# Attention of a decoder layer: scores of four heads at once, scores and maxima taking turns on three pairs of PSUM banks

## The chip, the cores and the metric

The kernel runs on one core of a Trainium2 chip. The metric is the device time of one execution in microseconds (us).

## The reference

One decoder layer on a batch of four sequences of 512 tokens with 512 features, in fp32. `ctx` has 512 tokens of 256 features.

```
q, k, v = heads(x @ Wq), heads(x @ Wk), heads(x @ Wv)            # 16 heads of 32
std  = softmax(q k^T / sqrt(32)) v
qa, ka = affinities(q), affinities(k)                            # 8 splats per head
w    = (qa * amplitudes) ka^T;  w = w / (sum(w) + 1e-8)
attn = ((1 - blend) * std @ Wo) + blend * (w v) @ Wo
x = layernorm(x + attn)
x = layernorm(x + ssm(ctx, z = x))      # conv, x_proj, softplus, scan over 512 steps with 16 states, gate silu(x)
x = layernorm(x + ffn(x))               # ternary weights, silu(gate) * up, rms norm, down
```

The affinities are sums of two exponentials of a token's distance to eight positions per head. Because w factors, `w v` is computed as qa times (ka^T v), one small product over all keys ("the affinities' product", L1319), with a denominator of its own (L1333).

## The kernel before

The four sequences ("batches" 0 to 3) are worked through one after the other, each in an attention phase and an FFN phase. A setup ahead of them quantises the FFN's weights. The state space scan of batch b + 1 doesn't depend on the attention; it is cut into 32 halves (state n, channel half a) that are spread over the phases. A half is two decays `dA = exp(A delta)` on ScalarE (`exp_dA`, L529), a product with B (L810), the scan (L818) and a product with C (L821) on VectorE (`scan_half`, L802), and a DMA of GpSimd's queue that accumulates into YA (L445). `slot_halves` (L257) says after which key tile of which head group how many halves stand. Outside the first batch a group of heads has two halves, behind key tiles 1 and 3, group 3 has three; in the first batch groups 0 to 2 have 3, 3 and 4.

The attention goes by head groups j = 0 to 3 of four heads (32 rows of the array each), and in each by key tiles kt = 0 to 3 of 128 keys. For a key tile TensorE makes the scores of all 512 queries against the 128 keys, keys on partitions. Softmax needs the maximum of each query, which lies across partitions. So the scores are computed twice. The *maxima product* (`max_scores`, L1187, matmuls L1201) of group (j, g) puts the scores of 128 queries g against all keys, queries on partitions, into banks 0 to 3, one bank to a head, all four heads on the four row groups of the array. VectorE reduces the four banks in one operation (`max_groups`, L869, L873). When four groups g of a head group are done, `transpose_max` (L1205, matmul L1208) turns the maxima into rows in bank 0, and ScalarE copies them negated into BR (`bias_row`, L574). The *score product* (`score_pair`, L1211) then makes the scores of two heads in banks 4 and 5 (L1214), and a product of a row of ones with BR subtracts the maxima (L1218). ScalarE takes the exponential of both banks into PT (L649). The *values products* (`values`, L1222, L1230) accumulate PT times V in bank 6 and PT times ones in bank 7, each of the four heads in its own 32 columns. At the end of a head group ScalarE inverts the sum by a logarithm and an exponential (`inverse_start`, L591), and VectorE normalises (`normalise`, L875).

Each engine's order is written out by hand, and engines wait for each other by semaphores. TensorE's order in a key tile is: pair 0, perhaps a maxima product, values into bank 6 of the key tile before, pair 1, values into bank 7, perhaps a maxima product. A pair waits for the exponential of the pair before, since both use banks 4 and 5. A maxima product waits for the reduction before. `GROUPS` (L271) says how many maxima groups of head group j + 1 are done ahead of each key tile of group j:

```
GROUPS = {0: (1, 2, 3, 4, 4), 1: (0, 2, 3, 4, 4), 2: (0, 1, 3, 4, 4), 3: (0, 0, 0, 0, 0)}
```

Before key tile 0 of group 2 (`KV_GROUP`) comes the affinities' product: the keys' affinities are transposed at the end of group 0 (L1352, bank 1), copied by ScalarE at the start of group 1 (L638), multiplied with V behind the second pair of group 2 (L1319, bank 1) and masked by VectorE (`splat_kv`, L921), for which the next maxima product waits, since bank 1 is its bank too. In group 3 there are no maxima. There TensorE makes the denominator (L1333, bank 0), transposes the next batch's context (L1161), makes its input projection (L1170) and the splat products for all queries (L1346, banks 0 and 1).

## Time and profile before

| | us |
|---|---|
| median of 3 executions (1514.86 to 1522.54) | 1519.27 |
| the profiled execution | 1525.26 |
| its span, first to last instruction | 1523.5 |
| TensorE busy (matmuls) | 1288.5 |
| VectorE busy | 1172.2 |
| ScalarE busy | 753.9 |
| GpSimd busy | 162.7 |

PE is TensorE, PEld its weight loads, DVE is VectorE, ACT is ScalarE, POOL is GpSimd, SP is SyncE. L12 is line 12 of the kernel. A multiplication of fp32 operands shows as two matmul records; overlapping records are counted once as busy time. "ps" is PSUM. The granted clock is TensorE's, as a part of 2.4 GHz; it has two levels, 1.0 and 0.5, and a stretch shows their mean.

### The profile page before, as it was taken

How to read it: one execution, taken by the hardware profiler on the slowest of the kernel's cores; microseconds unless marked ns; L12 is line 12 of the kernel's file. 1: busy time of each engine (PE TensorE's matmuls, PEld its weight loads, DVE VectorE, ACT ScalarE, POOL GpSimd, SP SyncE). 2: the span in 40 equal slices, each digit the busy share in tenths (PEclk: the TensorE clock that was granted, in tenths of full speed). 3: DMA queues.
4: the chain of work that ended last, by engine and by line, in shares of the span. 5: the costliest groups of instructions: out<-in, count | busy, mean ns of one | idle time of the engine just before them, and what ended most of it. 6: DMA issues, size and time to landing. Idle time of an engine off the chain costs nothing.

```text
span 1523.5 us, 15252 instructions
## 1 busy us (share of the span) xinstructions
PE 1288.5 (85%) x5466; PEld 556.9 (37%) x5466; DVE 1172.2 (77%) x1233; ACT 753.9 (49%) x1086; POOL 162.7 (11%) x211
## 2 busy tenths in 40 slices
PE   4673857979689999999899998999899998897896
PEld 3342312323245542223355432323354432223453
DVE  5877997977989997658789997656889997686323
ACT  6765434535466644335476644424477544442231
POOL 0000111100111121000101210000101210001001
PEclk9765988989789998689899997957799997989898
DMA  6854753434339862304159663222169662231131
GB/s 190 274 170 126 144 125 82 90 82 107 91 102 259 198 156 52 69 17 108 50 144 259 170 154 65 58 69 42 51 155 260 170 137 59 56 90 28 63 97 55
DMA packets 88987, 178.16 MB, mean 117 GB/s; under 512 B 11424, under 2 KB 22176, under 8 KB 88912
## 3 DMA queue, kind: packets, MB, share of 16 engines
q1 hardware_dynamic: 69664, 109.29, 24.0%
q0 software_dynamic: 18432, 67.12, 22.8%
q10 hardware_dynamic: 816, 0.79, 0.2%
q8 instruction: 43, 0.70, 0.2%
q14 instruction: 32, 0.26, 0.1%
HBM read 97.21 MB, written 12.85 MB: 72 GB/s over the span
## 4 chain that ended last, share of the span: by engine, by line
PE 48%; DVE 24%; ACT 7%; issue 7%; DMA 4%; POOL 1%; SPq 0%; DVEq 0%; POOLq 0%; ACTq 0%
PE ps L1413 8%; DVE ST L818 8%; PE ps L1214 8%; PE ps L1230 7%; PE ps L1201 4%; PE ps L1373 4%; DVE MX L873 4%; DVE ST L810 4%; PE ps L1357 3%; ACT PT L649 3%; DMA GU<-gu_tiles 2%; DMA WP<-proj_tiles 2%; PE ps L1292 2%; PE ps L1218 2%; PE ps L1170 2%
## 5 line engine op out<-in xcount | busy, mean ns | idle before, releaser
L818 DVE TENSOR_TENSOR_SCAN ST<-dA,ST 128x1024 f32<-128x1024 f32 x128 | 294.1, 2298 | 8.5 <-ACT dA L529 5.7
L649 ACT ACTIVATE PT<-ps 128x1024 f32<-128x1024 f32 x128 | 130.8, 1022 | 236.0 <-PE ps L1218 235.8
L1413 PE MATMUL ps<-V,GU 128*128 128x512 f16 x1024 | 239.3, 389 | 7.4 <-DVE V L1004 5.6
L445 POOL DMA_DIRECT2D YA<-ST x128 | 109.3, 854 | 1094.3 <-DVE ST L821 1030.3
L873 DVE TENSOR_REDUCE MX<-ps 128x4 f32<-128x2048 f32 x64 | 146.5, 2290 | 97.6 <-PE ps L1201 97.6
L529 ACT ACTIVATE dA<-DL,Aneg 128x511 f32<-128x511 f32 x256 | 169.3, 712 | 99.9 <-DVE ST L818 99.5
L1214 PE MATMUL ps<-QK 32*128 32x512 f32 x512 | 165.8, 727 | 35.9 <-ACT PT L649 32.5
L821 DVE TENSOR_TENSOR ST<-ST,BC 128x1024 f32<-128x1024 f32 x128 | 159.9, 1249 | 4.4
L810 DVE TENSOR_TENSOR ST<-DU,BC 128x1024 f32<-128x1024 f32 x128 | 155.8, 1218 | 0.0
L1373 PE MATMUL ps<-WP,HL 128*128 128x512 f32 x512 | 143.5, 424 | 9.8 <-DMA WP<-proj_tiles 9.4
L1413 PEld LDWEIGHTS ps<-V,GU 128*128 128x128 bf16 x1024 | 97.3, 100 | 144.5 <-issue 31.5
L1292 PE MATMUL ps<-XA,W 128*128 128x512 f32 x256 | 116.3, 608 | 10.2 <-ACT PT L618 10.1
L1218 PE MATMUL ps<-BR,one_row 1*128 1x512 f32 x256 | 119.5, 925 | 0.0
L1373 PEld LDWEIGHTS ps<-WP,HL 128*128 128x128 f32 x512 | 98.2, 194 | 38.6 <-issue 12.2
L1214 PEld LDWEIGHTS ps<-QK 32*128 32x128 f32 x512 | 48.2, 213 | 142.9 <-ACT PT L649 97.1
L1201 PE MATMUL ps<-QK 32*128 32x512 f32 x512 | 84.7, 732 | 18.0 <-DVE MX L873 11.4
L1030 DVE TENSOR_TENSOR QAK<-QAK,ps 128x512 f32<-128x512 f32 x64 | 43.7, 684 | 66.5 <-PE ps L1413 66.5
L1230 PE MATMUL ps<-PT,ones 128*32 128x512 f32 x512 | 83.2, 728 | 0.0
L1230 PE MATMUL ps<-PT,V 128*32 128x512 f32 x512 | 82.1, 718 | 0.5
L699 ACT CAST HL<-QAK 128x512 fp32r<-128x512 f32 x64 | 39.5, 617 | 80.8 <-DVE QAK L1030 80.8
L1292 PEld LDWEIGHTS ps<-XA,W 128*128 128x128 f32 x256 | 48.5, 194 | 76.8 <-issue 62.2
L709 ACT ACTIVATE QAK<-ps 128x512 f32<-128x512 f32 x64 | 38.0, 593 | 59.2 <-PE ps L1413 59.0
(230 smaller groups left out, 1560.6 us busy)
## 6 DMA issues: line engine op xcount, KB each, us to landing
YA<-ST POOLq DMA_DIRECT2D x128, 512.0 KB, 7.1
BC<-bc_rows SPq DMA_DIRECT2D x64, 512.0 KB, 5.4
GU<-gu_tiles SPq DMA_DIRECT2D x64, 256.0 KB, 8.1
WP<-proj_tiles SPq DMA_DIRECT2D x64, 256.0 KB, 7.2
ST<-in_L_ffn_w_gate_up_dram SPq DMA_DIRECT2D x16, 256.0 KB, 3.3
gu_tiles<-BC SPq DMA_DIRECT2D x16, 256.0 KB, 2.1
proj_tiles<-HL SPq DMA_DIRECT2D x16, 256.0 KB, 2.2
XIN<-in_x_dram SPq DMA_DIRECT2D x4, 1024.0 KB, 8.5
```

Source lines behind the costliest of these rows:

```text
L529: last = nc.scalar.activation(dA[:, a, e, 1:S], DL[:, 2 * a + e, 1:S], ACT.Exp, scale=Aneg[:, 2 * a + e, n:n + 1])
L649: nc.scalar.activation(PT[:, kt % 2, 2 * p:2 * p + 2, :], ps[:, 4:6, :], ACT.Exp, scale=SCALE).then_inc(s_exp, 1)
L810: nc.vector.tensor_tensor(ST[:, ring(bb, n, a), :, :], DU[:, 2 * a:2 * a + 2, :], BC[:, n % 2, 0:1, :].broadcast_to((P, 2, S)), ALU.mult). ...
L818: nc.vector.tensor_tensor_scan(flat, dA[:, a, :, :].rearrange("p e s -> p (e s)"), flat, 0.0, ALU.mult, ALU.add).then_inc(s_scan, 1)
L821: nc.vector.tensor_tensor(st, st, BC[:, n % 2, 1:2, :].broadcast_to((P, 2, S)), ALU.mult).then_inc(s_prod, 1)
L873: nc.vector.tensor_reduce(MX[:, g, 0:P:D], ps[:, 0:HG, :], AX_X, ALU.max).then_inc(s_mx, 1)
L1214: mm(ps[:, score_bank(h), :], QK[rows, 1, j, kt * P:(kt + 1) * P], QK[rows, 0, j, :], start=True, stop=False, tile_position=(D * h, 0))
L1218: last = mm(ps[:, score_bank(h), :], one_row[row, :], BR[row, j % 2, :], start=False, stop=True, tile_position=(D * h, 0))
L1230: last = mm(ps[D * h:D * h + D, bank, :], w, PT[:, kt % 2, h, :], start=(kt == 0), stop=(kt == KT - 1), tile_position=(0, D * h))
L1292: last = mm(bank, W[:, z, k, j * P:(j + 1) * P], XA[:, k, :], start=(k == 0), stop=(k == KT - 1))
L1373: last = mm(ps[:, 4 + r, :], HL[:, 2 * z + t % 2, r * P:(r + 1) * P], WP[:, t % 2, :], start=(t == 0 and z == 0), stop=(t == NT - 1 and z ...
L1413: last = mm(ps[:, f % F_RING, :], GU[:, t % GU_RING, k, m * P:(m + 1) * P], XHL[:, z, k, :], start=(k == 0 and z == 0), stop=(k == KT - 1 ...
```

## The change

In head groups 0 to 2 the scores of four heads are made in one go, in four banks ("quad"), in place of two pairs. Scores and maxima take turns on three pairs of banks, (0, 1), (2, 3), (4, 5), in the order of a list `TURNS`; a turn waits for the reader of the turn three before it. There is exactly one maxima group (of four products) to each key tile, always the fifth ahead; the reduction is split into two, one for each pair of banks, except for group 0. The transposed maxima and the transposed keys take a turn too. The keys are transposed in the last key tile of group 2, where no maxima group is left, and copied at the start of group 3. The affinities' product moves from group 2 to group 3, behind the denominator. In the last group pairs stay in banks 4 and 5. Where a group has three or four halves (the first batch), they stand one behind each key tile.

```diff
             if j < NG - 1:
-                third = max(1, len(mine) // 3)
-                return [[], mine[:third], [], mine[third:]]
+                extra = max(0, len(mine) - 3)
+                if len(mine) < 3:
+                    return [[], mine[:1], [], mine[1:]]
+                return [mine[:extra]] + [[h] for h in mine[extra:]]
...
+        GROUPS_AHEAD = 1
+        def group_in(j, kt):
+            n = KT * (j + 1) + kt + GROUPS_AHEAD
+            return divmod(n, KT) if n < KT * NG else None
+
+        PAIRS = ((0, 1), (2, 3), (4, 5))
+        TURNS = [("max", 1, 0, 0), ("max", 1, 0, 1)]
+        for j in range(NG - 1):
+            for kt in range(KT):
+                TURNS += [("score", j, kt, 0), ("score", j, kt, 1)]
+                if kt == KT - 1:
+                    TURNS.append(("turn", j + 1, 0, 0))
+                if group_in(j, kt):
+                    TURNS += [("max", *group_in(j, kt), 0), ("max", *group_in(j, kt), 1)]
+                else:
+                    TURNS.append(("keys", 0, 0, 0))
+        def pair(kind, j, i, part):
+            return PAIRS[TURNS.index((kind, j, i, part)) % 3]
...
# ScalarE
+                    if j == NG - 1:
+                        act.wait_ge(s_kat, b + 1)
+                        nc.scalar.copy(QAK[:, 2, :], ps[:, pair("keys", 0, 0, 0)[0], :]).then_inc(s_ka, 1)
                     if j > 0:
                         inverse_start(b, j - 1)
-                    if j == 1:
-                        act.wait_ge(s_kat, b + 1)
-                        nc.scalar.copy(QAK[:, 2, :], ps[:, 1, :]).then_inc(s_ka, 1)
...
# VectorE
-                    nc.vector.tensor_reduce(MX[:, g, 0:P:D], ps[:, 0:HG, :], AX_X, ALU.max).then_inc(s_mx, 1)
+                    if j == 0:
+                        nc.vector.tensor_reduce(MX[:, g, 0:P:D], ps[:, 0:HG, :], AX_X, ALU.max).then_inc(s_mx, 2)
+                        continue
+                    for part in range(2):
+                        bank = pair("max", j, g, part)[0]
+                        nc.vector.tensor_reduce(MX[:, g, 2 * D * part:2 * D * (part + 1):D], ps[:, bank:bank + 2, :],
+                                                AX_X, ALU.max).then_inc(s_mx, 1)
...
-                        if j == KV_GROUP and c == 0:
+                        if j > 0 and c == 0:
                             normalise(b, j - 1)
+                        if j == NG - 1 and c == 0:
                             splat_kv(b)
-                        lo, hi = GROUPS[j][c:c + 2]
-                        max_groups(b, j + 1, lo, min(lo + 1, hi))
-                        if j > 0 and j != KV_GROUP and c == 0:
-                            normalise(b, j - 1)
-                        max_groups(b, j + 1, lo + 1, hi)
+                        if j < NG - 1 and group_in(j, c):
+                            jm, g = group_in(j, c)
+                            max_groups(b, jm, g, g + 1)
...
# TensorE
+            def turn_free(b, kind, j, i, part):
+                before = TURNS.index((kind, j, i, part)) - 3
+                if before == -1:
+                    pe.wait_ge(s_dist, 2 * (b + 1))
+                    pe.wait_ge(s_pj2, 2 * (b + 1))
+                if before < 0:
+                    return
+                kind, j, i, part = TURNS[before]
+                if kind == "score":
+                    pe.wait_ge(s_exp, exps_done(b, j, i, part))
+                if kind == "max":
+                    pe.wait_ge(s_mx, maxima_done(b, j, i, part))
+                if kind == "turn":
+                    pe.wait_ge(s_br, NG * b + j + 1)
...
+            def score_quad(b, j, kt):
+                for part in range(2):
+                    turn_free(b, "score", j, kt, part)
+                if kt == 0:
+                    pe.wait_ge(s_br, NG * b + j + 1)
+                banks = quad("score", j, kt)
+                for h in range(HG):
+                    rows = slice(D * h, D * h + D)
+                    mm(ps[:, banks[h], :], QK[rows, 1, j, kt * P:(kt + 1) * P], QK[rows, 0, j, :],
+                       start=True, stop=False, tile_position=(D * h, 0))
+                for h in range(HG):
+                    row = slice(D * h, D * h + 1)
+                    last = mm(ps[:, banks[h], :], one_row[row, :], BR[row, j % 2, :],
+                              start=False, stop=True, tile_position=(D * h, 0))
+                last.then_inc(s_s, 2)
...
+                for j in range(NG - 1):
                     for kt in range(KT):
+                        score_quad(b, j, kt)
+                        if kt > 0:
+                            values(b, j, kt - 1, 6)
+                        if kt == KT - 1:
+                            transpose_max(b, j + 1)
+                        if group_in(j, kt):
+                            max_group(b, *group_in(j, kt))
+                        else:
+                            transpose_keys(b)
+                        if kt > 0:
+                            values(b, j, kt - 1, 7)
+                    for bank in (6, 7):
+                        values(b, j, KT - 1, bank)
```

`max_group` is `max_scores` for one group with the waits of `turn_free` for both of its pairs of banks; in it group (1, 0) waits for the bias row of group 0 as before. Group 3 keeps the old order of a pair, the values, a pair, the values, with the denominator and then the affinities' product behind the second pair of key tile 0.

## Rows read from the trace of the kernel before

**Rows 1.** The page, part 1: busy us (share of the span) xinstructions.

```profile
PE 1288.5 (85%) x5466; PEld 556.9 (37%) x5466; DVE 1172.2 (77%) x1233; ACT 753.9 (49%) x1086; POOL 162.7 (11%) x211
```

**Rows 2.** Windows, groups 0 to 2 of each batch: stretch, length, busy us, clock, DMA.

```profile
238.10:339.90 101.80, 81.73 (x451) 26.19 (x448) 81.62 (x57) 43.90 (x56) 10.54 (x11) 0.87 0.37 77
583.50:689.40 105.90, 96.79 (x450) 29.52 (x449) 64.03 (x45) 39.02 (x48) 6.42 (x7) 0.74 0.21 43
918.70:1024.70 106.00, 96.95 (x452) 29.25 (x448) 65.43 (x46) 38.95 (x48) 7.21 (x8) 0.74 0.27 61
1259.80:1351.40 91.60, 82.15 (x450) 26.33 (x450) 63.88 (x45) 39.03 (x48) 6.39 (x7) 0.87 0.25 50
```

**Rows 3.** Windows: group 1 of batches 1 and 2, parts of the first, group 3.

```profile
616.30:656.20 39.90, 38.70 (x151) 10.84 (x150) 21.92 (x15) 12.45 (x16) 2.57 (x3) 0.57 0.29 59
953.20:977.40 24.20, 22.78 (x151) 7.26 (x150) 18.83 (x12) 12.38 (x16) 1.70 (x2) 1.00 0.28 59
621.00:625.00 4.00, 3.74 (x14) 1.35 (x14) 3.97 (x5) 1.40 (x3) 0.00 (x0) 0.58 0.31 58
653.00:657.00 4.00, 4.00 (x22) 1.01 (x22) 0.00 (x0) 1.27 (x3) 0.00 (x0) 0.66 0.53 100
...
1024.70:1062.00 37.30, 35.94 (x126) 12.90 (x122) 26.70 (x27) 19.28 (x27) 2.55 (x3) 0.77 0.19 36
```

**Rows 4.** Timeline of all engines, end of group 2, high clock: start us, us, engine.

```profile
679.04 1.13 PE L1214 MATMUL ps<-QK 32*128 32x512 f32 x4
679.12 1.22 DVE L810 TENSOR_TENSOR ST<-DU,BC 128x1024 f32<-128x1024 f32 x1
...
680.33 1.07 PE L1230 MATMUL ps<-PT,ones 128*32 128x512 f32 x8
...
680.44 1.02 ACT L649 ACTIVATE PT<-ps 128x1024 f32<-128x1024 f32 x1 [1.45 <-PE ps L1218]
681.33 1.14 PE L1201 MATMUL ps<-QK 32*128 32x512 f32 x8
...
682.29 1.02 PE L1214 MATMUL ps<-QK 32*128 32x512 f32 x4
...
683.84 2.29 DVE L873 TENSOR_REDUCE MX<-ps 128x4 f32<-128x2048 f32 x1
...
686.96 0.66 PE L1208 MATMUL ps<-ident,MX 128*128 128x128 f32 x4
```

**Rows 5.** Timeline of TensorE, group 1 of batch 1, low clock.

```profile
641.57 2.09 PE L1201 MATMUL ps<-QK 32*128 32x512 f32 x8
643.44 1.92 PE L1214 MATMUL ps<-QK 32*128 32x512 f32 x4
...
645.71 1.94 PE L1230 MATMUL ps<-PT,V 128*32 128x512 f32 x8
647.58 2.08 PE L1214 MATMUL ps<-QK 32*128 32x512 f32 x4
```

**Rows 6.** Groups by line: names, shapes, count, busy us, mean ns, idle before and releasers.

```profile
L1214 PE MATMUL ps<-QK 32*128 32x512 f32 x512 | 165.8, 727 | 35.9 <-ACT PT L649 32.5
...
L1201 PE MATMUL ps<-QK 32*128 32x512 f32 x512 | 84.7, 732 | 18.0 <-DVE MX L873 11.4 <-DVE QAK L921 3.4 <-ACT BR L577 3.1
...
L1319 PE MATMUL ps<-V,QAK 128*128 128x512 f32 x32 | 24.3, 932 | 0.0
...
L879 DVE TENSOR_TENSOR X<-ps,RD 128x512 f32<-128x512 f32 x16 | 11.0, 689 | 36.3 <-ACT RD L596 36.3
...
L921 DVE SCALAR_TENSOR_TENSOR QAK<-ps,par,head_mask 128x512 f32<-128x512 f32 x4 | 3.0, 751 | 23.4 <-PE ps L1319 23.4
```

**Rows 7.** Timeline of VectorE, affinities in group 0 of batch 1.

```profile
602.80 0.87 DVE L890 TENSOR_SCALAR X<-X,par 128x512 f32<-128x512 f32 x2
...
606.20 1.22 DVE L810 TENSOR_TENSOR ST<-DU,BC 128x1024 f32<-128x1024 f32 x1
```

**Rows 8.** Timeline of TensorE, input projection in group 3 of batch 1.

```profile
703.21 3.70 PE L1170 MATMUL ps<-QAK,inT 128*128 128x512 f32 x8
```

More of the change, by code:

```diff
@@ L576, in bias_row @@
                 act.wait_ge(s_tm, NG * b + j + 1)
[L577 removed]
+                bank = pair("turn", j, 0, 0)[0] if j > 0 else 0
+                nc.scalar.mul(BR[:, j % 2, :], ps[:, bank, :], -1.0).then_inc(s_br, 1)
             def splat_exps(b):
@@ new lines, in max_group @@
+            def max_group(b, j, g):
+                if j == 0 and g == 0:
+                    pe.wait_ge(s_ev, 2 * KT * (b + 1))
+                    pe.wait_ge(s_q32, 2 * NG * b + UNITS.index((0, 1)) + 1)
+                    since(pe, s_br, NG * b)
+                if j == 0 and g > 0:
+                    pe.wait_ge(s_mx, maxima_done(b, 0, g - 1, 1))
+                if j == 1 and g == 0:
+                    pe.wait_ge(s_br, NG * b + 1)
+                banks = range(HG)
+                if j > 0:
+                    for part in range(2):
+                        turn_free(b, "max", j, g, part)
+                    banks = quad("max", j, g)
+                for h in range(HG):
+                    rows = slice(D * h, D * h + D)
+                    last = mm(ps[:, banks[h], :], QK[rows, 0, j, g * P:(g + 1) * P], QK[rows, 1, j, :],
+                              start=True, stop=True, tile_position=(D * h, 0))
+                last.then_inc(s_xs, 1)
@@ L1355, in out_products @@
+                for bank in (6, 7):
+                    values(b, j, KT - 1, bank)
                 def out_products(r, groups_of_heads):
```

123 lines of the change are left out of this document (51 added, 72 removed).

## The prediction, made before the changed kernel was built or run

> **What bounds the kernel now.** I read the page's first part, then the attention stretches by window, then instructions in order of time. TensorE is busy 85% of the span, VectorE 77% [rows 1]. The change touches head groups 0 to 3 of the four batches. Groups 0 to 2 (from the first score product of group 0 to that of group 3) last 101.8, 105.9, 106.0 and 91.6 us, 405.3 in all. VectorE works 275 us of them and TensorE 358, so TensorE comes first. The granted clock was 0.87, 0.74, 0.74 and 0.87 there [rows 2]. With only the levels 1.0 and 0.5 (2.4 and 1.2 GHz), the share at the low one is 2 x (1 - clock), weighted by length 40%.
>
> What the level costs is seen in two times group 1 ran: 24.2 us at 1.00, 39.9 at 0.57, with TensorE busy nearly throughout in both [rows 3]. At the high level a key tile is a full TensorE queue: a score pair to the next work 1.29 us, a values product 1.00, a maxima product 0.96, so 2 x 1.29 + 2 x 1.00 + 0.96 = 5.5 us [rows 4]. Both exponentials of a key tile read banks 4 and 5, so pair, 1.40 us to the exponential, its 1.02, next pair: 2.4 us, which values and maxima fill. At the low level a pair takes 2.27, a values product 1.87, a maxima product 1.87 [rows 5]: 2 x 2.27 + 3 x 1.87 = 10.2, with no slack.
>
> **The change, part by part.**
> *Pairs become quads.* Four heads occupy the four row groups at once, as the maxima product does now: eight records of four heads last 1.14 us, four records of two heads 1.13 [rows 4]; by line, 84.7 us for 64 maxima groups against 165.8 for 128 pairs [rows 6]. So a quad costs TensorE what one pair does: 1.2 us high, 2.27 low. The bias products of four heads are not in the trace; they cost no more than the pair's tail if they overlap, 0.25 more if not. I take the overlap, since the main product shows it. Per key tile this removes one pair, 1.29 or 2.27 us, in 48 key tiles. The Trainium skill (TensorE: Matmul & The Clock Gate, measured speedups of packing) has four row tiles at 3.07 times one, not 4; by that a quad would be some 0.15 us longer, an estimate, and the sum 7 us less good. The 0.96 us of a maxima product beside the two-head pair speaks for the full overlap.
>
> *The order becomes a ring.* The maxima lose their own four banks; scores and maxima alternate over three pairs of banks. A quad waits for the first half of the previous maxima group, a maxima product for the first exponential of its own key tile. One turn without a scan: half reduction, quad to exponential 1.40, exponential 1.02, maxima product to VectorE 1.20 (its 1.14 and a handover of 0.06) [rows 4]. The half reduction isn't in the trace: a full one takes 2.29 [rows 4]; half is 1.15 at least, 1.25 at most since other 128x1024 operations take 1.22. I take 1.22, two in 2.30 instead of 2.20. The turn is 1.22 + 1.40 + 1.02 + 1.20, with 0.1 of signals 4.94 us. TensorE's own work in it (quad 1.2, two values 2.1, maxima 1.0) is 4.3, so the ring decides. Where VectorE also scans a half (679.12 to 683.84, 4.72 [rows 4]) the turn is 2.30 + 4.72 = 7.0, and TensorE waits.
>
> Walked from first quad to first quad at the high level, two halves per group (batches 1 to 3):
> - Group 1, quad 0 at 0 us: VectorE ends the old scan at 3.9, normalises (three operations of 0.7 [rows 6]) to 6.0 and reduces the maxima product issued behind quad 0's exponential to 8.3. The first half of that frees quad 1 at 7.3; its exponential ends at 9.7, the maxima product is ready at 11.0, reduced at 13.2, and the scan behind it lasts to 17.9. Quad 2 starts at 12.2; its maxima product waits for VectorE from 15.9 to 17.9. Quad 3 starts at 19.2, its second exponential ends at 22.6. Meanwhile the transposition (0.66 [rows 4]) has run; now come the maxima product for the next group (1.0) and three values products (3.2): next quad 0 at 26.9. The second scan runs behind, 3.9 into the next group.
> - Group 0: no normalisation, but splat exponentials and affinities (602.80 to 606.20 on VectorE [rows 7], 3.4), and the first reduction waits for a scan, the second product for it; by the same steps 30.1.
> - Group 2: three maxima groups, in place of the fourth the key transposition, which needs only the first exponential: 26.0.
> Sum 83.0 for each of three batches. Batch 0 has 3, 3 and 4 halves: 30.1, 27.3 and, with a scan in each of four turns, 29.8, sum 87.2. The even spread of the halves helps there: three scans behind the last key tile now keep the maxima, transposition and next bias row waiting. In all 336 against 405: 69 us gained.
>
> *The affinities' product* leaves group 2 and lands in group 3 behind the first two pairs. There it lengthens TensorE's queue, full already: four full-height products took 3.70 in group 3 at the high level (L1170, eight records [rows 8]), at the low one 24.3 / 4 = 6.1 [rows 6]. VectorE's wait for it (23.4 in four batches [rows 6]) moves along and in part falls together with that for the denominator. I charge 3.6 x 4 = 14.5. Behind it are queued the next batch's context transpositions; ScalarE's copy of them, its two decays and the next exponentials wait for those in turn, so nothing covers it. The key transposition keeps its length (0.66); its copy moves from group 1 to the start of group 3, before the logarithm, under VectorE's scan.
> *VectorE* gets 48 more reductions, 0.1 each, already in the turns. DMAs don't change in number; batch 0's broadcasts and accumulations follow the moved halves and are due further apart. GpSimd's queue sees only that.
>
> High level throughout: 69 - 14.5 = 54.6 us gained. *The low level* makes TensorE the bound again: a key tile is 2.27 + 3 x 1.87 = 7.9 [rows 5], a group with its transposition some 32.5. Twelve groups come to 390, less 3 for the missing fourth product of group 2; 387 is 51 more than 336, and the moved product 11 more. With a share f of low time the gain is 54.6 - 62 f. I keep f = 0.4. For less: in the quads all row groups work, and the low stretch of group 1 ended only when transposition and four values products stood together without pairs (window 653 to 657 [rows 3]). For more: TensorE now waits 2 to 3 us behind each scan, and group 1 fell to 0.58 at 621 to 625 [rows 3] behind one short wait for a reduction. Gain 54.6 - 25 = 30. Sum: the profiled execution took 1525.3 (span 1523.5), 6.0 above the median of 1519.3; 1525.3 - 30 - 6 = **1489 us** on the scale of the medians.
>
> **The rivals.** 0.5% of this kernel is 7.6 us, about what a measurement can tell from no change.
> 1. *The clock stays high* because the products are denser: f near 0, gain 55, **1464**. For it: in batch 2 group 1 ran at 1.00 with TensorE 94% busy [rows 3]; against it: TensorE will be busy only 18 of 27 us.
> 2. *The ring is longer than walked*: each of 48 turns has four handovers, and two exponentials with a decay between them, or a quad at half overlap, can add 0.5 us per turn. Then 24 of the 30 are gone: **1513**; at 0.6 nothing is left. Against it: each link is a row; for it: I counted few signals. The Trainium skill (TensorEngine Tiling, PSUM Bottleneck) says that tiling speeds up the products but not the emptying of PSUM, and that this can become the limit. By it all of TensorE's 1.29 per key tile could be lost, the time 1519; the present rows, with VectorE idle a third of these stretches, don't show it yet.
> 3. *Slower: the clock stays low* through groups 0 to 3. It falls in the first wait behind a scan and isn't raised, since a group now has two such waits, and group 3, at 0.77 once already [rows 3], follows. Then 54.6 - 62 = -7, and the starts of group 0 and the wide products of group 3 add some 2 us each in four batches, -16: **1535**. It decides from f = 0.88 on. Against it: the longest low stretch of one group was 39.9 x 2 x 0.43 = 34 us and ended [rows 3], and at the low level TensorE has no pauses.
> The quads running two by two would give back the pair's 1.29 in 48 key tiles, 62 us, and also end slower; the maxima rows exclude nearly all of it.
>
> **How the numbers follow.** Forecast 0.46, rival 1 0.18, rival 2 0.20, rival 3 0.16. Faster by over 0.5% takes the forecast, rival 1 and a third of rival 2: 0.69. Within 0.5% the rest of rival 2 and a little of rival 3: 0.16. Slower 0.15. The range runs from rival 1 to the upper end of rival 2: 1464 to 1522; the forecast alone, with f from 0.2 to 0.6 (12 us either way), is 1477 to 1501.
>
> **What would show it.** Score and maxima products of 48 groups each with about 1.1 us per four heads; half reductions of 1.2 us, 96 of them; TensorE's idle time before quads released by the reduction and not by the exponential; turns without a scan near 5 us and with one near 7; groups 0 to 2 near 30, 27 and 26 us at a clock of 1.00; group 3 some 4 us longer. Wrong would be: a quad's bias products over 1.0 us, half reductions over 1.3, or a clock in groups 0 to 2 below 0.65.

## The result, and the profile after

The changed kernel takes **1524.25 us** (median of 20 executions, 1515.90 to 1530.43), the kernel before 1517.47 in 20 executions beside them (1496.52 to 1550.35). The two medians are 0.45% apart; the ratio is taken over the quicker executions of each kernel alone, since before has single slow ones up to 1550, and is 1.0095 (95% interval 1.0059 to 1.0130): slower by 0.95%. The prediction was 1489, faster, with a range up to 1522. It was wrong in its direction, and the time lies above its range.

The page of the changed kernel, its span, part 1 and the first two lines of part 4 (the chain; line numbers are those of the changed kernel: L1286 and L1290 are a quad's scores and bias products, L1257 the maxima product, L911 the half reduction, L907 the whole reduction of group 0, L1313 the values, L1268 the transposition of the maxima, L1414 the affinities' product):

```profile
span 1522.6 us, 15379 instructions
...
PE 1214.4 (80%) x5461; PEld 528.9 (35%) x5466; DVE 1174.1 (77%) x1281; ACT 750.3 (49%) x1086; POOL 162.7 (11%) x211
...
PE 34%; DVE 29%; issue 16%; DMA 5%; ACT 5%; POOL 1%; SPq 0%; DVEq 0%; POOLq 0%; ACTq 0%
```

The same chain in the kernel before:

```profile
PE 48%; DVE 24%; ACT 7%; issue 7%; DMA 4%; POOL 1%; SPq 0%; DVEq 0%; POOLq 0%; ACTq 0%
```

TensorE lost 74 us of busy time against [rows 1], and the span lost 0.9. TensorE's share of the chain fell from 48 to 34%; VectorE and "issue" took it over. The work was removed, and the end came hardly any sooner.

The windows of groups 0 to 2 of each batch, in the columns of [rows 2]:

```profile
239.63:333.92 94.29, 70.74 (x440) 19.95 (x441) 77.19 (x65) 42.95 (x56) 8.18 (x10) 0.75 0.37 79
586.80:681.28 94.48, 69.66 (x441) 20.46 (x441) 61.44 (x54) 37.72 (x48) 5.17 (x6) 0.78 0.26 58
921.35:1015.78 94.43, 69.60 (x440) 20.43 (x440) 61.45 (x54) 37.72 (x48) 5.09 (x6) 0.78 0.26 58
1255.85:1350.30 94.45, 69.60 (x441) 20.45 (x441) 61.45 (x54) 37.72 (x48) 5.11 (x6) 0.78 0.27 58
```

and the four groups of batch 1 one by one:

```profile
586.80:621.25 34.45, 25.47 (x148) 7.33 (x148) 18.38 (x20) 13.22 (x17) 0.87 (x1) 0.71 0.22 46
621.25:651.12 29.87, 22.20 (x152) 6.25 (x148) 20.51 (x18) 11.90 (x15) 1.72 (x2) 0.83 0.26 54
651.12:681.28 30.16, 21.99 (x149) 6.89 (x145) 22.56 (x18) 12.60 (x16) 2.58 (x3) 0.83 0.32 74
681.28:723.83 42.55, 39.25 (x159) 13.87 (x155) 27.43 (x28) 20.42 (x28) 2.59 (x3) 0.88 0.29 59
```

These stretches sum to 377.65 us, 27.7 less than the 405.3 of before, and the three later batches agree within 0.1 us, which those of before did not. So there is a gain; it was given back in two places.

*Group 3*, with the moved product, takes 41.1, 42.6, 42.6 and 31.7 us, together 158.0; before it took 36.9, 36.1, 40.7 and 31.6, together 145.2. That is 12.8 back. Not all of it is the product: group 3 ran at clocks of 0.92, 0.88, 0.88 and 0.95 here and of 0.95, 0.95, 0.79 and 0.78 before, and experiment 1 will show it at 39.5 us with the product in it.

*Ahead of group 0*. First TensorE, then VectorE, in order of time, around the first quad of batch 1:

```profile
580.48 0.66 PE L1268 MATMUL ps<-ident,MX 128*128 128x128 f32 x4
581.82 1.14 PE L1257 MATMUL ps<-QK 32*128 32x512 f32 x8 [0.69 <-ACT BR L609]
586.80 2.09 PE L1286 MATMUL ps<-QK 32*128 32x512 f32 x8 [3.84 <-DVE MX L911]
```

```profile
580.88 2.29 DVE L851 TENSOR_TENSOR_SCAN ST<-dA,ST 128x1024 f32<-128x1024 f32 x1
583.21 2.20 DVE L854 TENSOR_TENSOR ST<-ST,BC 128x1024 f32<-128x1024 f32 x1
585.33 2.34 DVE L911 TENSOR_REDUCE MX<-ps 128x2 f32<-128x1024 f32 x2
```

The list of turns begins with the two pairs of banks of maxima group (1, 0). The second pair of banks of quad (0, 0) is the fourth turn and takes the banks of the first, so the very first quad of a batch waits for the reduction of maxima that nobody needs yet. VectorE makes it only behind a scan and a product. From the transposition to the first score product it is 5.2 us in batch 0 and 6.3 in the others; before it was 2.8 and 2.55 (banks 4 and 5 were free then). That is 24.2 against 10.5: 13.7 back. The account closes: -27.7 + 12.8 + 13.7 = -1.2 us, and the two profiled spans are 1523.5 and 1522.6.

The groups by line show the wait's sum:

```profile
L911 DVE TENSOR_REDUCE MX<-ps 128x2 f32<-128x1024 f32 x96 | 113.0, 1219 | 107.8 <-PE ps L1257 107.8
L1286 PE MATMUL ps<-QK 32*128 32x512 f32 x384 | 75.6, 864 | 92.2 <-DVE MX L911 92.2
...
L1414 PE MATMUL ps<-V,QAK 128*128 128x512 f32 x32 | 18.6, 735 | 0.0
```

TensorE stood 92 us ahead of quads for the reduction, and VectorE 108 us ahead of the reduction for TensorE's product: each waits for the other, which is what a ring looks like. Lastly TensorE in group 1 of batch 1:

```profile
629.02 2.09 PE L1286 MATMUL ps<-QK 32*128 32x512 f32 x8 [4.04 <-DVE MX L911]
...
631.46 1.94 PE L1313 MATMUL ps<-PT,V 128*32 128x512 f32 x8
633.33 2.09 PE L1257 MATMUL ps<-QK 32*128 32x512 f32 x8
635.35 1.94 PE L1313 MATMUL ps<-PT,ones 128*32 128x512 f32 x8
637.22 1.38 PE L1286 MATMUL ps<-QK 32*128 32x512 f32 x8
```

Behind the 4.04 us of waiting the products run at the low level (2.09 where the high level shows 1.1), and they fill the turn without pause: 8.2 us from quad to quad, where my walk has 4.94.

### The profile page after: what moved, and what is told of

Read it like the earlier page. It is cut to its first block, busy times and chain, and to the rows that moved or that the text cites. A ratio compares the mean times of both kernels' runs of the same rounds, so it can differ in the third digit from the quotient of the medians.

```text
span 1522.6 us, 15379 instructions
## 1 busy us (share of the span) xinstructions
PE 1214.4 (80%) x5461; PEld 528.9 (35%) x5466; DVE 1174.1 (77%) x1281; ACT 750.3 (49%) x1086; POOL 162.7 (11%) x211
## 3 DMA queue, kind: packets, MB, share of 16 engines
q1 hardware_dynamic: 69664, 109.29, 24.2%
## 4 chain that ended last, share of the span: by engine, by line
PE 34%; DVE 29%; issue 16%; DMA 5%; ACT 5%; POOL 1%; SPq 0%; DVEq 0%; POOLq 0%; ACTq 0%
DVE ST L851 11%; PE ps L1489 8%; DVE ST L843 5%; PE ps L1449 4%; PE ps L1313 4%; DVE MX L911 3%; PE ps L1433 3%; DMA WP<-proj_tiles 3%; PE ps L1286 2%; PE ps L1297 2%; PE ps L1257 2%; PE ps L1208 2%; DVE ST L854 2%; DMA GU<-gu_tiles 2%; DVE BST L887 1%
## 5 line engine op out<-in xcount | busy, mean ns | idle before, releaser
L682 ACT ACTIVATE PT<-ps 128x1024 f32<-128x1024 f32 x128 | 125.8, 1021 | 227.2 <-PE ps L1290 187.2
L911 DVE TENSOR_REDUCE MX<-ps 128x2 f32<-128x1024 f32 x96 | 113.0, 1219 | 107.8 <-PE ps L1257 107.8
L1286 PE MATMUL ps<-QK 32*128 32x512 f32 x384 | 75.6, 864 | 92.2 <-DVE MX L911 92.2
L1489 PEld LDWEIGHTS ps<-V,GU 128*128 128x128 bf16 x1024 | 97.6, 100 | 144.5 <-issue 33.2
L1257 PE MATMUL ps<-QK 32*128 32x512 f32 x512 | 87.0, 753 | 22.6 <-ACT PT L682 19.9
L1313 PE MATMUL ps<-PT,V 128*32 128x512 f32 x512 | 84.9, 742 | 0.5
L732 ACT CAST HL<-QAK 128x512 fp32r<-128x512 f32 x64 | 39.5, 617 | 82.8 <-DVE QAK L1068 82.8
L1313 PE MATMUL ps<-PT,ones 128*32 128x512 f32 x512 | 74.2, 654 | 0.0
L1286 PEld LDWEIGHTS ps<-QK 32*128 32x128 f32 x384 | 21.0, 245 | 139.6 <-issue 139.6
L1372 PE MATMUL ps<-W,XA 128*128 128x512 f32 x128 | 57.7, 608 | 6.5 <-ACT V L641 5.7
```

The lines of the kernel that those rows point to most:

```text
L682: nc.scalar.activation(PT[:, kt % 2, 2 * p:2 * p + 2, :], ps[:, first_bank:first_bank + 2, :], ACT.Exp, scale=SCALE).then_inc(s_exp, 1)
L911: nc.vector.tensor_reduce(MX[:, g, 2 * D * part:2 * D * (part + 1):D], ps[:, bank:bank + 2, :], AX_X, ALU.max).then_inc(s_mx, 1)
L1257: last = mm(ps[:, banks[h], :], QK[rows, 0, j, g * P:(g + 1) * P], QK[rows, 1, j, :], start=True, stop=True, tile_position=(D * h, 0))
L1286: mm(ps[:, banks[h], :], QK[rows, 1, j, kt * P:(kt + 1) * P], QK[rows, 0, j, :], start=True, stop=False, tile_position=(D * h, 0))
L1313: last = mm(ps[D * h:D * h + D, bank, :], w, PT[:, kt % 2, h, :], start=(kt == 0), stop=(kt == KT - 1), tile_position=(0, D * h))
L1489: last = mm(ps[:, f % F_RING, :], GU[:, t % GU_RING, k, m * P:(m + 1) * P], XHL[:, z, k, :], start=(k == 0 and z == 0), stop=(k == KT - 1 ...
```

## The experiments

Edits are made to the changed kernel unless the text names the kernel before. Experiments 5 to 8 ran on another chip than 1 to 4 and 9 to 11, and 12 on a third, so medians of different experiments are compared with their profiles beside them. "Group" lengths run from the first score product of a group to that of the next.

**1. The first quad ahead of the first maxima.** The turns begin with quad (0, 0).

```diff
-        TURNS = [("max", 1, 0, 0), ("max", 1, 0, 1)]
+        TURNS = [("score", 0, 0, 0), ("score", 0, 0, 1), ("max", 1, 0, 0), ("max", 1, 0, 1)]
...
-                max_group(b, 1, 0)
                 for j in range(NG - 1):
                     for kt in range(KT):
                         score_quad(b, j, kt)
+                        if j + kt == 0:
+                            max_group(b, 1, 0)
```

> The changed kernel, with one edit: group 0's first quad takes the first two turns and is issued ahead of the maxima product (1, 0). Theory A (a wait that the prediction overlooked: the quad's second pair of banks waits for the first half reduction of (1, 0), which VectorE makes only behind a scan; 6.3 us from the transposed maxima to the first quad against 2.6 before): these distances fall back to 2.6 or less, in four batches some 14 us less than the changed kernel, 1524 to about 1510. Theory B (the start of group 0 is bound by VectorE anyway): the quad starts earlier, the second one doesn't, and the time stays at 1524 within 3.

Measured: 1508.53 us (1505.38 to 1515.86, 10 executions), 15.7 below the changed kernel; against before 1.0041 (1.0000 to 1.0082). TensorE at the same place:

```profile
574.71 0.66 PE L1269 MATMUL ps<-ident,MX 128*128 128x128 f32 x4
576.05 1.14 PE L1287 MATMUL ps<-QK 32*128 32x512 f32 x8 [0.69 <-ACT BR L610]
```

1.34 us in place of 6.3, and the quad now starts at the high level. The profiled spans differ by 19.3 us, and their stretches say where: 18.8 less ahead of the first quads, 6.7 more in the four groups 0 (36.0 us each, since the second quad and the maxima product ahead of it now wait for reductions), 1.0 more in groups 1 and 2, and 7.6 less in group 3, which the edit doesn't touch:

```profile
672.43:711.96 39.53, 36.25 (x158) 13.02 (x155) 27.24 (x28) 20.42 (x28) 2.59 (x3) 0.96 0.31 64
```

So the wait is on the path and is worth 12 us net; the rest is group 3 at 0.96 in place of 0.88. Why its clock was higher is not shown.

**2. The clock held up by products that are overwritten.** Full-height products of the identity with the queries go into the bank that the next quad overwrites: three behind key tile 0; behind key tile 2 five in group 0 and one in groups 1 and 2. They add work and change no output.

```diff
+                        if kt in (0, 2):
+                            turn_free(b, "score", j, kt + 1, 0)
+                            for _ in range(3 if kt == 0 else 5 if j == 0 else 1):
+                                mm(ps[:, pair("score", j, kt + 1, 0)[0], :], ident[:, :], QK[:, 0, j, :], start=True, stop=True)
```

> The changed kernel, plus products whose results are overwritten (a full-height product of 512 columns into the next quad's first bank), where TensorE waits behind a scan: three behind key tile 0, five behind key tile 2 of group 0 and one behind key tile 2 of groups 1 and 2. Theory C (the waits behind a scan drop the clock, and the turn without a scan that follows runs at 1.2 GHz, 8.2 us instead of 5): clock in groups 0 to 2 near 1.0 instead of 0.71 to 0.83, turns without a scan near 5 us, groups 0 to 2 of a batch 84 to 86 us instead of 94.5, the time some 30 us below the changed kernel. Theory D (the turns are long by themselves): the clock rises, the turns stay at 7 to 8 us, and the time doesn't fall.

Measured: 1489.94 us (1486.70 to 1495.88, 4 executions), 34 less, with 68 us of TensorE's work added; against before 0.9896 (0.9802 to 0.9990). Between the profiled executions groups 0 to 2 are 30.2 us shorter. Groups 0 to 2 of batch 1, and TensorE in the turn read above:

```profile
587.63:619.52 31.89, 28.10 (x165) 9.16 (x165) 18.39 (x20) 13.11 (x17) 0.87 (x1) 0.89 0.23 50
619.52:646.69 27.17, 22.09 (x160) 6.84 (x157) 20.49 (x18) 11.90 (x15) 1.72 (x2) 1.00 0.27 58
646.69:672.61 25.92, 21.37 (x157) 6.94 (x153) 22.55 (x18) 12.38 (x16) 1.72 (x2) 1.00 0.34 69
```

```profile
627.27 1.09 PE L1286 MATMUL ps<-QK 32*128 32x512 f32 x5 [1.26 <-DVE MX L911]
...
632.43 1.09 PE L1286 MATMUL ps<-QK 32*128 32x512 f32 x5 [0.43 <-DVE MX L911]
```

At a clock of 1.00 groups 1 and 2 take 27.2 and 25.9 us, and the turn 5.2. The walk had 26.9, 26.0 and 4.94. So the walk of these two groups was right, and what lies above it in the changed kernel is the clock. Theory C holds.

**3. The affinities' product over one key tile of four.** This leaves out three quarters of that product.

```diff
-                        for k in range(KT):
-                            last = mm(ps[:, 1, :], QAK[:, 2, k * P:(k + 1) * P], V[:, k, :], start=(k == 0), stop=(k == KT - 1))
+                        last = mm(ps[:, 1, :], QAK[:, 2, 0:P], V[:, 0, :], start=True, stop=True)
```

> The changed kernel with the affinities' product over one key tile instead of four (three quarters of it are left out, the output's splat part is not the reference's). Theory E (it lies bare in TensorE's queue in group 3): group 3 gets shorter by three products of 0.9 us at the high clock, 2.7 us a batch, 11 in all. Theory F (group 3 grew from 36 to 42.5 us for another reason, the late copy of the keys or the clock): under 4 us in all.

Measured: 1514.63 us (1503.90 to 1521.61, 10 executions), 9.6 less; against before 1.0013 (0.9973 to 1.0052). Group 3 of batch 1 is 38.63 where it was 42.55:

```profile
678.49:717.12 38.63, 35.33 (x153) 12.34 (x149) 27.42 (x28) 20.42 (x28) 2.59 (x3) 0.91 0.32 65
```

That is 3.9 us a batch. Three of the four products at the changed kernel's 18.6 / 4 = 4.65 us are 3.5, and the clock rose from 0.88 to 0.91. So the moved product has no cover, as priced.

**4. The scan's three operations set apart.** Product with B, scan and product with C no longer stand in one piece behind a reduction; they are spread behind the reductions of a group's four key tiles, outside batch 0 at most two behind one.

```diff
+        STEPS = {2: (0, 1, 2, 2, 3, 3), 3: (0, 1, 1, 2, 2, 3, 3, 3, 3), 4: (0, 0, 1, 1, 1, 2, 2, 2, 3, 3, 3, 3)}
...
+                        if j < NG - 1:
+                            mine = [h for chunk in halves for h in chunk]
+                            steps = [(step, h) for h in mine for step in (half_in, half_scan, half_out)]
+                            for at, (step, h) in zip(STEPS[len(mine)], steps):
+                                if at == c:
+                                    step(b, *h)
+                            continue
```

> The changed kernel, with the three operations of a half no longer in one block behind a reduction but one or two behind each (product with B, reduction, scan, reduction, product with C and the next half's product with B, reduction, scan, product with C) in groups 0 to 2. Theory C (the block of 4.7 us on VectorE makes the wait that drops the clock, and the ring has 2.6 us of room on VectorE in every turn): turns of 5 us all through, clock near 1.0, groups 1 and 2 of batches 1 to 3 near 23 us instead of 30, group 0 near 28 instead of 34; about 60 us below the changed kernel, near 1465. Theory D (the turns are long by themselves, or VectorE's sum binds): groups 1 and 2 stay above 27 us and the time above 1500.

Measured: 1490.11 us (1489.98 to 1490.65, 4 executions), 34 less, a little over half of what was expected; against before 0.9894 (0.9785 to 1.0002). Groups 0 to 2 of batch 1:

```profile
589.32:620.33 31.01, 24.78 (x148) 7.10 (x149) 19.29 (x21) 13.22 (x17) 0.87 (x1) 0.72 0.24 49
620.33:645.78 25.45, 19.81 (x152) 5.73 (x148) 20.31 (x18) 11.91 (x15) 1.72 (x2) 0.93 0.26 56
645.78:670.95 25.17, 20.09 (x149) 6.16 (x145) 20.44 (x17) 12.38 (x16) 1.72 (x2) 0.86 0.26 47
```

Each group is 3.4 to 5 us shorter (in batch 0, with its three and four halves, the sum is unchanged), but the clock is still 0.72, 0.93 and 0.86. Waits of 3.84 us ahead of the first quad of group 0, of 3.12 ahead of its last and of 2.8 ahead of the second quads of groups 1 and 2 (589.32, 612.10, 626.84, 652.28) are left, and the clock falls at or just behind each.

**5. The same in the kernel before**, with the even halves of the change but its own pairs, banks and order; the scan's operations are split as in experiment 4.

```diff
-                third = max(1, len(mine) // 3)
-                return [[], mine[:third], [], mine[third:]]
+                extra = max(0, len(mine) - 3)
+                if len(mine) < 3:
+                    return [[], mine[:1], [], mine[1:]]
+                return [mine[:extra]] + [[h] for h in mine[extra:]]
...
+        STEPS = {2: (0, 1, 2, 2, 3, 3), 3: (0, 1, 1, 2, 2, 3, 3, 3, 3), 4: (0, 0, 1, 1, 1, 2, 2, 2, 3, 3, 3, 3)}
```

> The kernel before, with the halves' three operations apart as in the changed kernel's version of that, and the changed kernel's even spread of the halves in batch 0. Theory G (spreading VectorE's steps helps whatever the scores do, since maxima products wait for VectorE there too): at least 15 us below the kernel before. Theory H (before, TensorE's queue is full and hides the scans; only the ring of the changed kernel needs the steps apart): within 8 us of the kernel before, so that the gain of 34 us belongs to the changed kernel's ring.

Measured: 1499.13 us (1491.24 to 1514.54, 4 executions). The kernel before, beside it on the same chip, had a median of 1540.06 with quickest executions of 1495.05 and 1499.41, which lie among those of this version, so no ratio can be stood on: neither theory is decided. In the profile group 0 is 2.6 to 4.2 us shorter (30.2, 30.3 and 30.7 in batches 1 to 3, before 32.8 to 34.4), groups 1 and 2 have their shorter lengths of before (24.3 and 33.2). The setting apart is worth something in the old order too, in group 0; how much in all is open.

**6. Only the affinities' product moved**, in the kernel before.

```diff
-        KV_GROUP = NG - 2
+        KV_GROUP = NG - 1
```

> The kernel before, with the affinities' product and VectorE's masking moved from group 2 to the start of group 3 behind its second pair, and nothing else. Theory E (the product costs TensorE the same in both places, and group 2 loses also the wait of the next maxima product for the masking): group 3 about 4 to 5 us longer a batch, group 2 6 to 9 us shorter, in all 8 to 20 us below the kernel before. Theory I (group 2 hides the product behind VectorE's scans, group 3 doesn't): group 2 shorter by less than 3 us, and the time above the kernel before.

Measured: 1512.78 us (1504.29 to 1538.00, 4 executions), within the spread of before. Groups 2 and 3 of batch 2:

```profile
996.92:1022.34 25.42, 22.82 (x153) 7.35 (x149) 20.24 (x14) 12.45 (x15) 1.70 (x2) 1.00 0.27 59
1022.34:1065.33 42.99, 38.07 (x158) 13.34 (x154) 28.91 (x30) 20.32 (x28) 3.39 (x4) 0.92 0.36 80
```

Group 2 falls to 25.4 us at a clock of 1.00. With the product in it, it has 33.2 at 0.90, and once 29.9 at 1.00 (experiment 11), so 4.5 to 7.8 us are saved. Group 3 rises by 2 to 9. In batches 0 and 1 of the same execution group 2 took 41.8 and 41.3 at clocks of 0.67 and 0.55, which hides the effect in the total. Neither theory's time can be told from the spread; group 2 did what Theory E says. This is also the old order at its quickest: groups 1 and 2 at 24.3 and 25.4 us, where the changed kernel with the clock held up has 27.2 and 25.9.

**7. Edits 1 and 4 together.**

```diff
+        TURNS = [("score", 0, 0, 0), ("score", 0, 0, 1), ("max", 1, 0, 0), ("max", 1, 0, 1)]
...
+        STEPS = {2: (0, 1, 2, 2, 3, 3), 3: (0, 1, 1, 2, 2, 3, 3, 3, 3), 4: (0, 0, 1, 1, 1, 2, 2, 2, 3, 3, 3, 3)}
```

> The changed kernel with both edits that helped by themselves: group 0's first quad first, and the halves' steps apart. If the two gains are independent (15.7 and 34.1 us), about 1474. If the quad's start only exposes the reductions of groups (1, 0) and (1, 1) behind it, group 0 gets longer by 2 to 4 us and the time is 1478 to 1490.

Measured: 1480.63 us (1469.28 to 1484.34, 4 executions), 43.6 below the changed kernel; the two parts alone gave 15.7 and 34.1. They nearly add, and the time lies in the expectation's second range, with group 0 up to 1.5 us longer than in experiment 4.

**8. Edits 1 and 4 with overwritten products** ahead of the first two maxima groups, behind key tile 2 of group 0 and behind key tile 0 of groups 1 and 2.

```diff
+                            turn_free(b, "max", 1, 0, 0)
+                            mm(ps[:, pair("max", 1, 0, 0)[0], :], ident[:, :], QK[:, 0, 0, :], start=True, stop=True)
                             max_group(b, 1, 0)
...
+                        if (j > 0 and kt == 0) or (j == 0 and kt == 2):
+                            turn_free(b, "score", j, kt + 1, 0)
+                            for _ in range(2):
+                                mm(ps[:, pair("score", j, kt + 1, 0)[0], :], ident[:, :], QK[:, 0, j, :], start=True, stop=True)
```

> As the version with both edits, plus overwritten full-height products where TensorE still waits at the start: one ahead of each of the maxima products (1, 0) and (1, 1), two behind key tile 2 of group 0, two behind key tile 0 of groups 1 and 2. Theory C (a wait of TensorE drops the clock, and the low stretch behind it costs): clock above 0.95 in groups 1 and 2 and above 0.9 in group 0, turns without a scan 5 us, group 0 near 28, groups 1 and 2 near 23, some 15 to 20 us below the version without these products, near 1457. Theory J (what is left is VectorE and the ring, not the clock): the clock rises and the time stays within 5 us of it.

Measured: 1444.74 us (1441.74 to 1446.05, 4 executions), 79.5 below the changed kernel and 36 below experiment 7, more than Theory C's 15 to 20; between the two profiles 27 lie in groups 0 to 2 and 10 in group 3. Groups 0 to 3 of batch 1:

```profile
575.93:603.94 28.01, 23.42 (x164) 7.10 (x164) 24.36 (x24) 14.22 (x19) 3.00 (x3) 1.00 0.27 56
603.94:628.03 24.09, 20.19 (x157) 6.18 (x153) 20.31 (x18) 11.91 (x15) 1.72 (x2) 1.00 0.31 67
628.03:650.87 22.84, 19.47 (x152) 6.26 (x148) 20.43 (x17) 12.38 (x16) 1.72 (x2) 1.00 0.28 56
650.87:688.71 37.84, 34.58 (x159) 12.44 (x155) 28.04 (x29) 20.43 (x28) 3.46 (x4) 1.00 0.44 99
```

All four are at 1.00 here, also group 3, which no edit touched: 37.8 in place of 42.6. In the next batch the groups ahead of it are at 1.00 too, and yet it is longer:

```profile
958.49:997.97 39.48, 36.21 (x159) 13.08 (x155) 28.22 (x29) 20.43 (x28) 3.39 (x4) 0.96 0.42 95
```

Over the versions of the changed kernel with the whole product, group 3 of batches 0 to 2 mostly has one of four lengths, near 37.8 us at 1.00, 39.5 at 0.96, 42.6 at 0.88 and 44.4 at 0.85. Which one falls to a batch does not follow from the clock of the groups ahead of it, and is open.

**9. The changed kernel with pairs in place of quads**, in the same turns, so that only the product of four heads at once is undone.

```diff
                 for part in range(2):
                     turn_free(b, "score", j, kt, part)
-                for h in range(HG):
+                    for h in (2 * part, 2 * part + 1):
...
-                last.then_inc(s_s, 2)
+                    last.then_inc(s_s, 1)
```

> The changed kernel without its quads: two heads and their bias rows, then the other two, each pair as soon as its own pair of banks is free, in the same turns. Theory K (TensorE's work isn't what sets the pace of groups 0 to 2 any more; the ring of reduction, score, exponential and maxima product does, and a quad joins it at its later half): TensorE does 1.3 us more in each of 48 key tiles (62 us), and the time is within 12 us of the changed kernel's 1524, perhaps below, since the first pair starts earlier and TensorE idles less. Theory L (the saving of the quads is real and the moved waits only hide it): 30 to 60 us above the changed kernel.

Measured: 1523.00 us (1509.31 to 1527.16, 10 executions), ratio to before 1.0114 (1.0065 to 1.0163): the time of the changed kernel (1524.25), with TensorE busy for 50 us more:

```profile
PE 1264.5 (83%) x5466; PEld 550.4 (36%) x5466; DVE 1174.4 (77%) x1281; ACT 752.0 (49%) x1086; POOL 163.0 (11%) x211
```

Groups 0 to 2 of batch 1:

```profile
585.75:621.34 35.59, 28.77 (x148) 8.75 (x149) 22.11 (x23) 13.38 (x17) 2.99 (x3) 0.76 0.21 46
621.34:651.87 30.53, 25.17 (x153) 7.61 (x149) 20.49 (x18) 12.22 (x15) 1.72 (x2) 0.83 0.23 52
651.87:681.85 29.98, 24.62 (x148) 7.95 (x144) 22.57 (x18) 12.81 (x16) 2.48 (x3) 0.83 0.32 73
```

Groups 1 and 2 of the four batches last 239.2 us, with quads 240.3: the quads' saving isn't on the path of this order. Elsewhere larger differences cancel. The first pair of a batch has banks 4 and 5 free and waits 2.55 us in place of 6.3 (14 less in all), the four groups 0 are 8 us longer, and the stretches outside, group 3 included, 7 longer. This is what rival 2 cited from the Trainium skill (TensorEngine Tiling (Array Packing), PSUM Bottleneck): tiling speeds up the products and not the emptying of PSUM. By that rule this run should show TensorE's time saved and the kernel's not, and groups 1 and 2 do; but what the ring stands behind is here also VectorE's scan, which empties no bank (experiment 4).

**10. Pairs with edits 1 and 4**, the counterpart of experiment 7.

```diff
+        TURNS = [("score", 0, 0, 0), ("score", 0, 0, 1), ("max", 1, 0, 0), ("max", 1, 0, 1)]
...
+                    for h in (2 * part, 2 * part + 1):
```

> The version with group 0's first scores first and the halves' steps apart (1480.6 us), with pairs in turns in place of quads. Theory K: within 10 us of 1481 or below. Theory L, now that VectorE's blocks are gone and TensorE's work is nearer to the pace: 25 to 60 us above.

Measured: 1468.19 us (1460.71 to 1474.73, 4 executions), ratio to before 0.9687 (0.9631 to 0.9743), and 12 below the same kernel with quads. Theory K holds: the quads gain nothing here either. That they cost time this run doesn't show. Of the 13.8 us between the profiled executions only 4.1 lie in groups 0 to 2; 8.0 lie in group 3, where the two kernels are the same, and the two sets of four executions overlap (1460.71 to 1474.73, 1469.28 to 1484.34).

**11. The kernel before once more**, unchanged, for a second profile.

> The kernel before, unchanged, for a second profile beside the first (span 1523.5 us). Theory M (its spread of 1496 to 1558 us comes from the level of the clock in single head groups, which falls in one execution and not in another): the same groups differ from the first profile by whole steps of 12 to 20 us at a clock of 0.55 to 0.6 against 1.00, while the other stretches agree within 1 us a batch. Theory N (the spread is in the FFN or the DMAs): groups 0 to 3 agree within 5 us in all.

Measured: 1514.05 us. Group 1 of batch 1, then groups 0 and 1 of batch 3:

```profile
620.50:644.46 23.96, 22.53 (x150) 7.27 (x149) 18.83 (x12) 12.15 (x15) 1.72 (x2) 1.00 0.27 60
...
1233.39:1273.51 40.12, 38.18 (x147) 11.05 (x144) 23.94 (x19) 14.12 (x18) 3.84 (x4) 0.57 0.25 54
1273.51:1311.75 38.24, 37.03 (x150) 10.55 (x149) 20.32 (x13) 12.49 (x16) 1.71 (x2) 0.60 0.19 41
```

In the first profile group 1 of batch 1 had taken 39.9 us at 0.57 [rows 3] and group 1 of batch 3 24.0 at 1.00. Here it is the other way round. Groups 1 and 2 of before have a short and a long length, 14 to 16 us apart, and executions differ in which of them fall into the long one. (Group 0 has 34.4 and, here, 40.1; behind a long group 1, group 2 was 29.9 at 1.00.) Every stretch between these groups, group 3 included, agrees with the first profile within 2 us, so Theory M holds in the main.

**12. Pairs with everything of experiment 8.**

```diff
+                    for h in (2 * part, 2 * part + 1):
...
+                        if (j > 0 and kt == 0) or (j == 0 and kt == 2):
+                            turn_free(b, "score", j, kt + 1, 0)
```

> The fastest version so far (first quad first, steps apart, overwritten products against the clock's fall; 1444.7 us), with pairs in turns in place of its quads. Theory K (the quads' saving never lies on the path): within 6 us of 1445, as the clock is held high in both. Theory L (with the clock high and VectorE's blocks gone, TensorE's work is the pace: a key tile of pairs is 5.6 us, the ring 4.94): groups 1 and 2 get longer by up to 0.65 us in each of 36 key tiles, 23 us or more with the overwritten products, near 1470.

Measured: 1432.78 us (1427.72 to 1437.37, 4 executions), ratio to before 0.9448 (0.9380 to 0.9516), the fastest version: 5.5% below before and 12 us below experiment 8, further than Theory K's 6. Its groups 0 to 2 of batch 1:

```profile
573.92:600.81 26.89, 26.10 (x164) 8.08 (x164) 24.35 (x24) 14.54 (x19) 3.00 (x3) 1.00 0.25 53
600.81:623.62 22.81, 21.49 (x156) 6.98 (x153) 20.31 (x18) 12.02 (x15) 1.72 (x2) 1.00 0.37 73
623.62:645.59 21.97, 20.77 (x152) 7.07 (x148) 20.32 (x17) 12.49 (x16) 1.72 (x2) 1.00 0.32 57
```

Each is 0.9 to 1.3 us shorter than with quads (28.0, 24.1, 22.8), at the same clock; over all batches groups 0 to 2 are 13.7 us shorter, which is nearly the whole difference of the two profiled executions, 15.7. So here the quads do cost time. The timeline of all engines at its second key tile of group 1:

```profile
605.95 2.35 DVE L925 TENSOR_REDUCE MX<-ps 128x2 f32<-128x1024 f32 x2
606.37 1.13 PE L1307 MATMUL ps<-QK 32*128 32x512 f32 x4
...
607.22 1.13 PE L1307 MATMUL ps<-QK 32*128 32x512 f32 x4
607.77 1.94 ACT L684 ACTIVATE PT<-ps 128x1024 f32<-128x1024 f32 x2 [2.40 <-PE ps L1311]
```

The first pair starts 0.42 us into the reduction, since the turn three before it is an exponential and only the second pair's is a reduction. With quads (experiment 8) the product stood 1.37 us behind the reduction's start (609.07 to 610.44): a quad waits for the later of its two banks' readers.

## Why the prediction was wrong

The forecast was a gain of 30 us and 6 of the profiled execution's excess; measured is a loss of 6.8 between medians, or a gain of 0.6 between profiled executions. By its own steps:

**The costs of the operations held.** The half reduction was taken as 1.22 us and is 1.219. From the quad to the next product it is 1.30 (627.27 to 628.57 in experiment 2's trace), as for a pair to its next work (1.29), so a quad does cost TensorE what a pair does; the 1.2 charged was 0.1 low. The turn without a scan is 5.2 for 4.94. Groups 1 and 2 without the low level are 27.2 and 25.9 for 26.9 and 26.0. For group 0 the walk's 30.1 was not seen at 1.00 in its own form; it is 31.9 at 0.89 and 34.4 as built. The moved product was charged 14.5 and group 3 grew by 12.8, but that near match is part luck, since the clocks of group 3 differ between the two profiles. At nearly the same clock it is 36.1 us without the product (before, batch 1, 0.95) and 39.5 with it (experiment 1, 0.96), 3.4 for 3.6 charged.

**Failed step 1: "Walked from first quad to first quad".** The walk began at the first quad of group 0 and used "the first reduction waits for a scan" inside it. It never asked what the first quad itself waits for: its second pair of banks is turn 4, and the turn three before it is that same reduction behind the same scan. It cost 13.7 us between the profiles; experiment 1 gets 18.8 back there and pays 6.7 in group 0.

**Failed step 2: "With a share f of low time the gain is 54.6 - 62 f".** The share was right (f = 0.4; measured 2 x (1 - 0.77) = 0.46 in groups 0 to 2), the price was not. I spread the difference between a wholly low and a wholly high group evenly over it. But the low time isn't spread: it comes with each long wait and lasts into the turn without a scan, where TensorE has little slack to lose: 8.2 us for 5.2 in experiment 2. The groups lasted 377.65 for 336 walked, 41.7 more, where 51 f gives 23 at the measured share. Experiment 2 returned 30.2 of the 41.7 by holding the clock. That the clock falls in the scan waits was rival 3's mechanism, correctly placed; I had expected it to matter only from f = 0.88 on.

**Failed step 3: "405.3 in all", and 6.0 subtracted.** I took the gain against groups that in that execution included long low stretches which come and go. Taking for each group of the first profile the length it has without one (34.0, 24.7, 43.2 in batch 0; 34.4, 24.0, 33.2 in the others) gives 376.7, the 377.65 of the changed kernel. So against a kernel before without long groups, groups 0 to 2 gain nothing; the change gains by not having the long mode, and loses 13.7 and 12.8. The fastest of the 20 executions of before, 1496.5, plus these two is 1523.0, near the 1524.25 measured; that this execution had no long group is likely, but it has no profile. The profiled execution of before lay 8 above the median of 20, with two long groups in it (39.9 and 47.4) worth 30 us, so its excess was a draw and not an offset to subtract.

**Failed step 4: "Per key tile this removes one pair, 1.29 or 2.27 us, in 48 key tiles", from "so TensorE comes first".** TensorE was 88% busy there, and the removed pairs were what the change was to gain by. But in the new order the path at the high level runs through reduction, scan and exponential, as my own turn of 4.94 over TensorE's 4.3 said. The walk even gave group 1 26.9 us, where [rows 3] had 24.2 at the same level, and I didn't compare the two. Measured at 1.00, groups 1 and 2 are 27.2 and 25.9 in the new order and 24.3 and 25.4 in the old one with the product moved (experiment 6). Experiment 9 shows the quads to be worth nothing in groups 1 and 2, experiment 12 shows them to cost 12 us once the clock and the scans are out of the way. Rival 2 said that a longer ring would take the gain; its cause (handovers, half a microsecond per turn) was not the one found.

Two sums of the prediction are off without bearing on this. A third of rival 2 is 0.07, so "faster" adds up to 0.71, not 0.69. And 1.29 us in 48 key tiles are 62 us, which taken off the forecast's gain give 1551, not rival 2's 1519.

Three parts of the change are thus settled. The quads gain nothing, and cost 12 us where nothing else holds the ring. The moved product costs 3.4 us a batch in group 3 and returned 4.5 to 7.8 in group 2 of the old order. The order of the turns loses 14 us in one place. The even halves of batch 0 were not tried alone.

## What to carry to other kernels

When buffers are handed round in turns (a ring), check the first turns after every joint with the work ahead: whoever comes there waits for a reader that nobody hurried. Merging two products into one also merges their waits; keep them apart if one of the two banks comes free earlier. And before counting an operation's removal as gain, undo it in thought in the new order: if the order is bound by other waits, it is worth nothing, while splitting the long block that the ring stands behind (here a scan of three operations) was worth 34 us. Last, before counting a gain from a profile, look whether its stretches repeat: here one profile of before held 30 us that other executions don't have.

## What the runs showed of the hardware that was not expected

- TensorE's granted clock in the changed kernel fell in waits of 3.8, 5.7 and 4.0 us (the ones that end at 586.80, 612.24 and 629.02 in batch 1) and was high again 5 to 13 us behind them. 68 us of overwritten full-height products in such waits brought 1.00 in groups 1 and 2 of batches 1 to 3 and took 34 us off the time.
- In the kernel before, group 1 of batch 1 ran at 0.57 with TensorE 97% busy (39.9 us, [rows 3]) in one execution and at 1.00 with 94% (23.96 us, experiment 11) in another. In the first the clock fell at 621.6, behind a wait of only 1.14 us, and stayed low for 34 us although TensorE hardly paused.
- Two profiles of before differ by 11 us, 9 of them in groups 0 to 2. This is the likely source of the spreads, though most executions have no profile: 1496.5 to 1550.4 us in 20 executions of before, 1515.9 to 1530.4 in 20 of the changed kernel, 1490.0 to 1490.7 in the 4 of experiment 4. Three executions could not have told that 1519 is a mixture.
